# Attended rows kept in DRAM per batch element, loaded whole, and cut into output tiles during the split

## The chip, the cores and the metric

The kernel runs on one core of a Trainium2 chip. The core has a matrix engine (TensorE, "PE" in the profile; "PEld" is its weight load), a vector engine (VectorE, "DVE"), a scalar engine (ScalarE, "ACT"), GpSimd ("POOL") and SyncE ("SP"), which here only issues DMAs. Sixteen DMA engines move the data; everything that SP issues goes to them through one queue (q1), what POOL issues through another (q0). The metric is the time on the device in microseconds (us); lower is better.

## What is computed

A layer norm of `x` (32 batch elements of 56 rows, 512 wide), a cross attention of these rows over a context of 1500 rows and the 56 rows themselves (16 query heads, 4 key and value heads, 96 wide), its output projection with `Wo`, a residual sum, and a mixture of 8 experts of which each row takes 2:

```python
def _L0_xattn_ref(latents, context, Wq, Wk, Wv, Wo):   # latents: layer norm of x
    hidden = jnp.concatenate([context, latents], axis=1)
    q = (latents @ Wq.T).reshape(b, q_len, H, HD)       # 32 x 56 rows, H 16, HD 96
    k = (hidden @ Wk.T).reshape(b, s_len, KV, HD)       # KV 4
    v = (hidden @ Wv.T).reshape(b, s_len, KV, HD)
    ...
    out = jnp.einsum('bkgqs,bksd->bkgqd', attn, v)
    out = out.reshape(b, H, q_len, HD).transpose(0, 2, 1, 3).reshape(b, q_len, H * HD)
    return out @ Wo.T

def _L0_ffn_ref(x, W_gate, b_gate, W_e, b_e):           # x: layer norm of the sum
    _, top_idx = jax.lax.top_k(x @ W_gate + b_gate, 2)
    y_all = jax.nn.relu(jnp.einsum('bsd,edh->bseh', x, W_e) + b_e)
    return jnp.take_along_axis(y_all, top_idx[..., None], axis=2).mean(axis=2)
```

## The kernel before

All products are made from fp32 values split in two: a high part (a cast to a reduced type, written by ACT or POOL) and a low part (the value less its high part, written by DVE or POOL). Three matrix products of such parts stand for one.

The program has four stages, one after the other, with all engines meeting between them:

1. **project** (line 218): the layer norm of `x` and the products for queries, keys and values of the rows, stored to DRAM.
2. **attend** (line 491): a loop over the 32 batch elements. PE projects the context to keys and values, makes scores and weighs the values. The result of an element goes to DRAM unscaled. While the next element is at work it is brought back, POOL multiplies it with the inverse sums (`normalize`, line 198), and `store_att` (line 206) writes it to the scratch tensor `att_t`. The result on the chip is laid out 96 partitions (one for each place d in a head) by 16 heads by 56 rows. `att_t` has 1536 lines (head and d) of 1792 columns (all rows of all elements), so the store cuts a partition into 16 runs of 56 numbers: 1536 pieces of 224 bytes. At the end of the stage POOL splits the first of the output tiles (lines 650 to 654).
3. **combine** (line 1008): the output projection. The 1792 rows are taken in 14 tiles of 128 (`OT`), which do not line up with the elements of 56 rows. `load_rows` (line 213) brings a tile: 128 partitions by 12 blocks by 128 columns, 1536 pieces of 512 bytes, 768 KB. ACT writes its high part (line 1180), DVE its low part (line 1207), and PE makes 36 products for a tile (line 1295, `output`). In the middle of tile t PE also transposes the normed rows of tile t-1 (line 1279), and then makes their gate logits (line 953).
4. **experts** (line 1330): the rows, gathered by expert, go through the experts' weights.

What sets the order around the change is the code of stage 3, one list for each engine:

- SP, for every t: the load of tile t+2; then two stores of tile t-1 (`store_rows`, line 1320), the sum `x1` (line 1324) and the normed rows `xn` (line 1327); for some t a part of an expert's weights (line 1062, 640 KB); then, when the sum of tile t is made, rows of `x` (line 1056). All of it is in one queue. At t = 12 SP issues four loads of the late part of the experts' weights (line 978) and then the bias of all experts, spread over 128 partitions (line 1098, 2 MB). After the loop it waits until all token numbers are in DRAM and loads the table of them (line 1103).
- DVE, for every t: sum and statistics of tile t, its normed rows (line 938), the places of the tokens of tile t-1, the low part of tile t+2 (line 1207), the gate of tile t. There is one buffer for normed rows: line 938 of tile t waits until the store of tile t-1 has landed (`xn_stored`).
- POOL: the split of the early part of the experts' weights (lines 1149 and 1154), and two scatters for each of 12 tiles, which write the token numbers to DRAM by q0 (line 1161).
- The first tile lies in the homes of `wv` and `wk`, the even tiles in `raw`, the odd ones in `att`.

## Time and profile before

| | us |
|---|---|
| median of 3 runs (lowest, highest) | 3391.51 (3391.44, 3392.01) |
| time of the profiled execution | 3390.29 |
| its span, first to last instruction | 3388.4 |
| PE busy | 3341.6 (99% of the span) |
| DVE / ACT / POOL busy | 2052.6 / 1648.8 / 1051.4 |
| PE idle, all stretches with a named releaser | 40.4 |

Stage 3 runs from 3065 to 3215 us of the span, and the experts' first product starts at 3233. All times in the text are microseconds from the start of the span. The clock of PE has two levels, 2.4 and 1.2 GHz; in the views they are 1.00 and 0.50, and a number between is a mean over the stretch. A busy PE is not at its peak, since matmuls overlap in the records.

### The profile page before, as it was taken

The page shows a single profiled execution, that of the slowest core. Times are in us where ns is not written, and L with a number is a line of the kernel's source. Part 1 is how long each engine was busy: PE and PEld are TensorE (multiplying, and loading weights), DVE is VectorE, ACT ScalarE, POOL GpSimd, SP SyncE. Part 2 cuts the span into 40 slices and gives each one's busy share as a digit, 9 for nine tenths or more (in the row PEclk, how much of TensorE's full clock was granted, in tenths as well). Part 3 has the DMA queues.
Part 4 walks back from the last instruction along what each step waited for, and adds up shares of the span by engine and source line. Part 5 has one row for each costly group of instructions (what it writes and reads, how often), then busy time and mean ns, then how long its engine had stood idle before and what let it go on. Part 6 is the DMA issues. An engine that isn't in the chain of part 4 may idle for free. (4 is left out here: it accounts for less than half of the span.)

```text
span 3388.4 us, 64330 instructions
## 1 busy us (share of the span) xinstructions
PE 3341.6 (99%) x21610; PEld 3107.7 (92%) x21610; DVE 2052.6 (61%) x2995; ACT 1648.8 (49%) x3146; POOL 1051.4 (31%) x865
## 2 busy tenths in 40 slices
PE   8999999999999999999999999999999999998989
PEld 8989999999999999999999999999999999997777
DVE  5346666666666666666666666666666666665645
ACT  3225555555555555555555555555555555552232
POOL 0032223332333333332222222233323333326554
PEclk9999999999999999999999999999999999999989
DMA  6542222222212122222222222222222121226865
GB/s 229 198 144 59 59 65 65 65 61 61 63 46 60 56 63 65 64 65 64 65 65 59 65 57 60 65 65 65 61 61 61 47 61 55 63 75 164 195 194 188
DMA packets 307512, 282.96 MB, mean 84 GB/s; under 512 B 200634, under 2 KB 257546, under 8 KB 307338
## 3 DMA queue, kind: packets, MB, share of 16 engines
q1 hardware_dynamic: 301738, 266.10, 27.6%
q0 software_dynamic: 5728, 16.27, 1.5%
q8 instruction: 26, 0.43, 0.1%
q14 instruction: 20, 0.16, 0.0%
HBM read 208.33 MB, written 73.96 MB: 83 GB/s over the span
## 5 line engine op out<-in xcount | busy, mean ns | idle before, releaser
L822 PE MATMUL ps_proj<-wv_hi,parts 128*125 128x384 f32 x3072 | 875.6, 339 | 0.0
L767 DVE TENSOR_TENSOR probs_lo<-probs,probs_hi 125x448 fp32r<-125x448 f32 (+1 forms) x896 | 682.0, 778 | 275.7 <-ACT probs_hi L694 263.2
L809 PE MATMUL ps_proj<-parts,wk_hi 128*128 128x500 f32 x2304 | 711.1, 390 | 2.9 <-DVEq L722 2.9
L822 PEld LDWEIGHTS ps_proj<-wv_hi,parts 128*125 128x125 f32 x3072 | 560.0, 185 | 5.8
L147 POOL TENSOR_SCALAR parts<-raw 128x1000 fp32r<-128x1000 f32 (+1 forms) x198 | 238.3, 1204 | 957.2 <-PE ps_proj L822 777.8
L686 ACT ACTIVATE probs<-ps_scores 125x448 f32<-125x448 f32 (+1 forms) x896 | 463.0, 517 | 121.6 <-PE ps_scores L870 78.8
L822 PE MATMUL ps_proj<-wv_lo,parts 128*125 128x384 f32 x1536 | 518.4, 338 | 0.0
L809 PEld LDWEIGHTS ps_proj<-parts,wk_hi 128*128 128x128 f32 x2304 | 431.4, 188 | 91.6 <-DVEq L722 3.2
L673 ACT CAST values_hi<-ps_proj 125x384 fp32r<-125x384 f32 x384 | 184.4, 480 | 645.3 <-PE ps_proj L822 645.3
L694 ACT CAST probs_hi<-probs 125x448 fp32r<-125x448 f32 (+1 forms) x896 | 484.1, 540 | 28.3
L736 DVE TENSOR_TENSOR values_lo<-ps_proj,values_hi 125x384 fp32r<-125x384 f32 x384 | 214.3, 558 | 431.6 <-ACT values_hi L673 428.9
L870 PE MATMUL ps_scores<-queries_hi,keys_lo 104*125 104x224 f32 (+1 forms) x1664 | 454.6, 273 | 0.0
L865 PE MATMUL ps_scores<-queries_hi,keys_hi 96*125 96x224 f32 (+1 forms) x1664 | 452.3, 272 | 0.0
L866 PE MATMUL ps_scores<-queries_lo,keys_hi 96*125 96x224 f32 (+1 forms) x1664 | 451.8, 272 | 0.0
L888 PE MATMUL ps_attended<-probs_hi,values_hi 125*97 125x224 f32 x1664 | 447.5, 269 | 2.0 <-DVE probs_lo L767 1.6
L809 PE MATMUL ps_proj<-parts,wk_lo 128*128 128x500 f32 x1152 | 448.5, 389 | 0.0
L889 PE MATMUL ps_attended<-probs_hi,values_lo 125*96 125x224 f32 x1664 | 442.6, 266 | 0.0
L890 PE MATMUL ps_attended<-probs_lo,values_hi 125*97 125x224 f32 x1664 | 442.3, 266 | 0.0
L202 POOL TENSOR_TENSOR probs<-probs 96x448 f32<-96x448 f32 x31 | 35.7, 1152 | 1209.7 <-DMA probs<-inverse_sums 1209.7
L667 ACT CAST keys_hi<-ps_proj 96x500 fp32r<-96x500 f32 x288 | 164.9, 573 | 501.6 <-PE ps_proj L809 501.6
L727 DVE TENSOR_TENSOR keys_lo<-ps_proj,keys_hi 96x500 fp32r<-96x500 f32 x288 | 192.8, 670 | 336.6 <-ACT keys_hi L667 336.2
L870 PEld LDWEIGHTS ps_scores<-queries_hi,keys_lo 104*125 104x125 f32 (+1 forms) x1664 | 306.5, 184 | 2.3
(218 smaller groups left out, 5822.7 us busy)
## 6 DMA issues: line engine op xcount, KB each, us to landing
raw<-in_ctx SPq DMA_DIRECT2D x192, 500.0 KB, 3.6
qk_hi<-proj_out_hi SPq DMA_DIRECT2D x60, 224.0 KB, 2.0
qk_lo<-proj_out_lo SPq DMA_DIRECT2D x60, 224.0 KB, 2.4
queries_hi<-qk_hi SPq DMA_DIRECT2D x32, 336.0 KB, 3.5
queries_lo<-qk_lo SPq DMA_DIRECT2D x32, 336.0 KB, 3.6
att_raw<-attended SPq DMA_DIRECT2D x128, 84.0 KB
probs<-att_raw SPq DMA_DIRECT2D x31, 336.0 KB, 5.7
probs<-inverse_sums SPq DMA_DIRECT2D x31, 336.0 KB, 3.0
```

Of the source, the lines that this page charges most:

```text
L147: pool.tensor_scalar(hi, raw, 1.0, 0.0, ALU.mult, ALU.add).then_inc(stream["hi"], 1)
L686: act.activation(pr[0:R, u % PRING, 0:N], psc[0:R, u % SBANKS, 0:N], ACT.Exp, scale=SCALE).then_inc(exp_done, 1)
L694: act.copy(prs[0][0:R, u % PRING, 0:N], pr[0:R, u % PRING, 0:N]).then_inc(p_hi, 1)
L767: dve.tensor_tensor(prs[1][0:R, u % PRING, 0:N], pr[0:R, u % PRING, 0:N], f(prs[0][0:R, u % PRING, 0:N]), ALU.subtract).then_inc(p_lo, 1)
L809: mm = pe.matmul(pproj[n % 2][:, 0:CS], w["wk"][a][:, j // 3, i * P:(i + 1) * P], ct[v][:, c, j // 3, :], start=(j == 0), stop=(j == 3 * K ...
L822: mm = pe.matmul(pproj[n % 2][0:VT, 0:KD], ct[a][:, t // VTC, j // 3, s], w["wv"][v][:, j // 3, :], start=(j == 0), stop=(j == 3 * KT - 1))
L865: pe.matmul(o, kt[0][:, h, s], q[0][0:HD, c], start=True, stop=False)
L866: pe.matmul(o, kt[0][:, h, s], q[1][:, c], start=False, stop=False)
L870: mm = pe.matmul(o, kt[1][:, h, s], q[0][:, c], start=False, stop=True)
L888: pe.matmul(o, vt_hi[:, t, h], hi, start=(t == 0), stop=False)
L889: pe.matmul(pav[0:HD, h % 2, 0:GQ], vt_lo[:, t, h], hi, start=False, stop=False)
L890: mm = pe.matmul(o, vt_hi[:, t, h], lo, start=False, stop=(t == NVT))
```

## The change

Each element's attended rows are kept in DRAM as they lie on the chip: `att_t` becomes 32 blocks of 96 by 896 numbers, and `store_att` writes 96 pieces of 3584 bytes. `load_element` reads a block as one run of 86016 numbers, cut into 128 partitions of 672 (128 pieces of 2688 bytes, 336 KB). The index of the sum in the output product thereby has another order (d before head), and the host puts `Wo` in the same order; its load keeps its shape. A tile of 128 rows now takes columns of three or four elements (`segments`), so every split writes its tile with three or four instructions. For tiles 1 to 13 that is 41 high parts on ACT and 41 low parts on DVE where there were 13 each; for tile 0 POOL has three of each where it had one and three.

Six slots for elements take the place of the two for tiles: four in `raw`, two in `att`. Tile 0 needs elements 0 to 2 (loaded to the homes of `wv`), tile 1 elements 2 to 4; element 4 goes to a place of its own first, in the area of the experts' raw weights, since `raw` is still in use. Elements 2 and 4 are loaded twice. In SP's loop the load of tile t+2 becomes the loads of the elements whose slots the splits up to tile t have set free: four at t = 0, three at t = 3, 6 and 10, one at t = 11, two at the others. At t = 12 the bias is issued ahead of the four late loads, and these wait for the split of tile 13 where they waited for that of tile 12, since tile 13 now lies partly in `raw`.

```diff
-    sp.dma_start(scratch["att"].rearrange("(h d) (b q) -> b d h q", d=HD, q=Q)[b],
-                 home[0].rearrange("d (h q) -> d h q", q=Q)).then_inc(stream["att_stored"], 16)
-def load_rows(sp, scratch, t, att, loaded):
-    sp.dma_start(att, scratch["att"].rearrange("(k p) r -> p k r", p=P)[:, :, bass.ds(t * P, P)]).then_inc(loaded, 16)
+    sp.dma_start(scratch["att"][b], home[0]).then_inc(stream["att_stored"], 16)
+def load_element(sp, scratch, e, home, loaded):
+    rows = scratch["att"][e].rearrange("d c -> (d c)").rearrange("(p c) -> p c", p=P)
+    sp.dma_start(home, rows).then_inc(loaded, 16)
+def segments(t):
+    return [(e, lo - e * Q, min(t * P + P, e * Q + Q) - lo, lo - t * P)
+            for e in range(t * P // Q, (t * P + P - 1) // Q + 1) for lo in (max(t * P, e * Q),)]
+def last_tile(e):
+    return (e * Q + Q - 1) // P
+def of_element(home, q, n):
+    return home.rearrange("p (k q) -> p k q", q=Q)[:, :, q:q + n]
...
-                load(1)
+                load(2)
+                load(3)
+                load_element(sp, scratch, 4, fourth, fourth_loaded)
                 load_x(0)
...
                         if t == 0:
                             sp.wait_ge(stream["lo"], (B + 1) * LOADS)
-                        if t + 2 == OT - 1:
-                            sp.wait_ge(stream["att_stored"], START + B * 16)
-                        load(t + 2)
+                            for e in range(4, ERING + 2):
+                                load(e)
+                        for e in range(ERING + 2, B):
+                            if last_tile(e - ERING) == t:
+                                if e == B - 1:
+                                    sp.wait_ge(stream["att_stored"], START + B * 16)
+                                load(e)
...
                     if t == OT - 2:
-                        sp.wait_ge(a_lo, START + OT - 2)
+                        sp.wait_ge(g["e_lo"], E)
+                        sp.dma_start(g["area"][:, 0:E * D], io["be"].broadcast_to([P, E * D])).then_inc(g["bias_loaded"], 16)
+                        sp.wait_ge(a_lo, START + OT - 1)
                         for e in range(LATE_RING):
                             load_late(sp, g, io, e)
-                        sp.wait_ge(g["e_lo"], E)
-                        sp.dma_start(g["area"][:, 0:E * D], io["be"].broadcast_to([P, E * D])).then_inc(g["bias_loaded"], 16)
...
-                    act.copy(ats[0][t % 2], att[t % 2]).then_inc(a_hi, 1)
+                    for e, q, n, c in segments(t):
+                        op = act.copy(ats[0][t % 2][:, :, c:c + n], rows_of(t, e, q, n))
+                    op.then_inc(a_hi, 1)
...
-                    dve.tensor_tensor(ats[1][t % 2], att[t % 2], f(ats[0][t % 2]), ALU.subtract).then_inc(a_lo, 1)
+                    for e, q, n, c in segments(t):
+                        op = dve.tensor_tensor(ats[1][t % 2][:, :, c:c + n], rows_of(t, e, q, n), f(ats[0][t % 2][:, :, c:c + n]), ALU.subtract)
+                    op.then_inc(a_lo, 1)
```

How it moves SP's DMAs, first at t = 2 and 3. Here `raw<-att_t` and `att<-att_t` are loads of tiles (before) or elements (after), `x1_rows` and `xn_rows` the two stores, `raw_then_bias<-in_we` an expert's early weights. Before:

```order
L1056 DMA x_rows<-in_x 128x512
L215 DMA att<-att_t 128x12x128
L1324 DMA x1_rows<-x1 128x512
L1327 DMA xn_rows<-xn_g 128x512
L1062 DMA raw_then_bias<-in_we 128x1280
```

And after:

```order
L1083 DMA x_rows<-in_x 128x512
L217 DMA raw<-att_t 128x672 x2
L217 DMA att<-att_t 128x672
L1365 DMA x1_rows<-x1 128x512
L1368 DMA xn_rows<-xn_g 128x512
L1089 DMA raw_then_bias<-in_we 128x1280
```

Three loads of 336 KB stand ahead of the stores where one of 768 KB stood. Next, SP at t = 12 and after it; `raw<-in_we` are late loads, `raw_then_bias<-in_be` is the bias. Before:

```order
L1327 DMA xn_rows<-xn_g 128x512
L978 DMA raw<-in_we 128x768 x4
L1098 DMA raw_then_bias<-in_be 128x4096
L1327 DMA xn_rows_dense<-xn_g 128x512
L1103 DMA id_table<-token_ids 104x128
L978 DMA raw<-in_we 128x768 x2
```

And after:

```order
L1368 DMA xn_rows<-xn_g 128x512
L1127 DMA raw_then_bias<-in_be 128x4096
L998 DMA raw<-in_we 128x768 x4
L1368 DMA xn_rows_dense<-xn_g 128x512
L1136 DMA id_table<-token_ids 104x128
L998 DMA raw<-in_we 128x768 x2
```

The bias has moved ahead of the four late loads. Last, DVE at t = 1, between the places of the tokens and the gate. Before:

```order
L1223 TENSOR_TENSOR cumulated<-cumulated,selected_sum 128x8
L1207 TENSOR_TENSOR att_lo<-att,att_hi 128x1536
L1228 TENSOR_REDUCE expert_of_block<-masks 128x1
```

And after:

```order
L1264 TENSOR_TENSOR cumulated<-cumulated,selected_sum 128x8
L1247 TENSOR_TENSOR att_lo<-raw,att_hi 128x12x8
L1247 TENSOR_TENSOR att_lo<-raw,att_hi 128x12x56
L1247 TENSOR_TENSOR att_lo<-att,att_hi 128x12x56
L1247 TENSOR_TENSOR att_lo<-att,att_hi 128x12x8
L1269 TENSOR_REDUCE expert_of_block<-masks 128x1
```

One subtraction of 1536 numbers for each partition has become four, of 96, 672, 672 and 96.

## Rows read from the trace of the kernel before

**Rows 1.** Waits of PE over the whole span: waiter, releaser: us, times, longest.

```profile
PE ps_table L1580 <- DMA id_table<-token_ids: 8.6, 1, 8.6
PE ps_t L1279 <- DVE xn_g L938: 7.6, 4, 4.9
PE ps_t L1560 <- DMA x_gathered<-xn_rows,index: 5.9, 2, 5.6
PE ps_proj L809 <- DVEq L722: 2.9, 1, 2.9
```

**Rows 2.** Windows (length; busy PE PEld DVE ACT POOL; PE clock, DMA share, GB/s): five tiles.

```profile
3085.91:3096.93 11.02, 10.02 (x52) 8.20 (x50) 7.14 (x19) 2.36 (x3) 8.88 (x9) 1.00 1.01 328
...
3107.39:3124.59 17.20, 12.27 (x52) 9.95 (x50) 6.00 (x17) 2.25 (x3) 3.96 (x5) 0.80 0.98 198
...
3134.68:3145.74 11.06, 10.06 (x52) 8.19 (x50) 6.05 (x21) 2.26 (x3) 4.74 (x4) 1.00 0.72 110
3145.74:3155.66 9.92, 9.92 (x51) 8.27 (x50) 5.88 (x19) 2.25 (x3) 0.16 (x1) 1.00 0.87 171
3155.66:3166.31 10.65, 10.00 (x51) 8.19 (x50) 5.98 (x17) 2.36 (x3) 10.01 (x9) 1.00 0.87 295
```

**Rows 3.** Timeline of PE after its longest wait of stage 3: start, us, idle before.

```profile
3117.03 1.12 PE L1279 MATMUL ps_t<-ident_g,xn_g 128*128 128x128 f32 x4 [4.93 <-DVE xn_g L938]
```

**Rows 4.** The chain that ended last, 3083 to 3222: start, us, what.

```profile
3083.21 7.68 DMA xn_rows<-xn_g
...
3101.77 14.53 DMA xn_rows<-xn_g
...
3129.31 10.35 DMA xn_rows<-xn_g
...
3148.82 11.47 DMA xn_rows<-xn_g
...
3209.81 11.98 DMA token_ids<-token_ids_f,places
```

**Rows 5.** Timeline of SP's queue at t = 3, load of a tile and store of normed rows.

```profile
3099.98 0.43 SPq L215 DMA_DIRECT2D att<-att_t  x1
...
3101.77 0.33 SPq L1327 DMA_DIRECT2D xn_rows<-xn_g  x1
```

**Rows 6.** Windows of single stretches, columns as in rows 2.

```profile
3086.20:3088.00 1.80, 1.80 (x11) 1.51 (x10) 1.29 (x2) 0.00 (x0) 1.62 (x2) 1.00 1.09 317
...
3224.00:3226.00 2.00, 0.76 (x4) 0.52 (x4) 0.74 (x5) 0.37 (x1) 0.00 (x0) 0.50 1.00 373
...
3109.00:3116.00 7.00, 3.10 (x15) 2.28 (x13) 0.35 (x3) 1.67 (x2) 0.00 (x0) 0.93 1.01 95
...
3150.00:3155.00 5.00, 5.00 (x30) 4.24 (x29) 1.97 (x6) 0.59 (x1) 0.00 (x0) 1.00 0.60 55
```

**Rows 7.** DMA issues, stores of attended rows: count, KB each, median us to landing.

```profile
att_t<-probs SPq DMA_DIRECT2D x31, 336.0 KB, 3.7
```

**Rows 8.** Groups of instructions of stage 3 by form: count, busy us, mean ns.

```profile
L1207 DVE TENSOR_TENSOR att_lo<-att,att_hi 128x1536 fp32r<-128x1536 f32 x7 | 12.3, 1751 | 0.2 <-ACT att_hi L1180 0.2
L1207 DVE TENSOR_TENSOR wk_lo<-raw,wk_hi 128x1536 fp32r<-128x1536 f32 x6 | 11.9, 1981 | 0.8 <-ACT wk_hi L1180 0.8
...
L1180 ACT CAST att_hi<-att 128x1536 fp32r<-128x1536 f32 x7 | 10.3, 1472 | 8.8 <-DMA att<-att_t 8.7
...
L1238 DVE TENSOR_TENSOR over<-ps_table,of_m 128x96 f32<-128x96 f32 x1 | 0.2, 250 | 0.0
```

**Rows 9.** Timeline of SP's queue at the end of stage 3.

```profile
3201.48 2.32 SPq L978 DMA_DIRECT2D raw<-in_we  x4
3203.84 0.54 SPq L1098 DMA_DIRECT2D raw_then_bias<-in_be  x1
...
3221.81 0.33 SPq L1103 DMA_DIRECT2D id_table<-token_ids  x1
```

**Rows 10.** Timeline of DVE: low parts of the last late weights.

```profile
3229.32 1.85 DVE L1004 TENSOR_TENSOR parts<-raw,parts 128x768 fp32r<-128x768 f32 x2 [0.92 <-ACT parts L998]
```

More of the change, by code:

```diff
@@ L604, in _ @@
                 sp.wait_ge(att_stored, START + (B - 1) * 16)
-                load_rows(sp, scratch, 0, first, first_loaded)
+                for e, *_ in segments(0):
+                    load_element(sp, scratch, e, first[e], first_loaded)
                 load_wo(sp, stream, io, RAW)
@@ L1024, in combine @@
         wo = stream["wo"]
-        att = [stream["rows"], sb("att", [P, HT, P])[:]]
+        two = sb("att", [P, 2 * ELEMENT])
+        slots = [(two, i - 2) if i in (2, 3) else (stream["rows"], (i + 2) % ERING) for i in range(ERING)]
+        slots = [x[:, n * ELEMENT:(n + 1) * ELEMENT] for x, n in slots]
         ats = [[home, sb(f"att_{n}", [P, HT, P], F32R)[:]] for home, n in zip(stream["first_parts"], ("hi", "lo"))]
         w_raw = g["area"][:, 0:2 * EARLY_W].rearrange("p (n c) -> p n c", n=2)
+        fourth = g["area"][:, EARLY_W:EARLY_W + ELEMENT]
         home = [g["area"][0:HD, 2 * EARLY_W + i * H * Q:2 * EARLY_W + (i + 1) * H * Q] for i in range(2)]
@@ L1034, in combine @@
         pcnt = g["ptab"][:, 0:E]
-        loaded = [sem(f"rows_loaded{i}") for i in range(2)]
+        loaded, fourth_loaded = [sem(f"element_loaded{i}") for i in range(ERING)], sem("fourth_loaded")
         small_loaded, consts = g["small_loaded"], sem("consts_g")
@@ L1051, in _, with load @@
             def _(sp):
-                def load(t):
-                    load_rows(sp, scratch, t, att[t % 2], loaded[t % 2])
+                def load(e):
+                    load_element(sp, scratch, e, slots[e % ERING], loaded[e % ERING])
                 def load_x(t):
```

30 lines of the change are left out of this document (19 added, 11 removed).

## Prediction

> **What bounds the kernel now.** I read the waits of PE first. PE is busy for 99% of the span (the table), so only what PE waits for, or what it does at its lower clock, can be won. In stage 2, where the loop over 32 elements runs, there is one wait of 2.9 us, at its start, and none that has to do with the store of the attended rows [rows 1]. What is done to that store gives nothing there. Three waits lie where the change works: 7.6 us in four pieces, before the transposes of the normed rows in stage 3 (line 1279), 8.6 us for the table of token numbers after stage 3, and 5.9 us for the first gathered rows [rows 1].
>
> The windows of single tiles show what the four waits cost. A tile without one takes 9.92 us. Tiles 2, 4, 6 and 8 take 11.02, 17.20, 11.06 and 10.65 [rows 2], which is 1.10, 7.28, 1.14 and 0.73 more, 10.25 in sum. Tile 4 costs more than its wait of 4.93 us [rows 3]: its mean granted clock is 0.80 where the others have 1.00 [rows 2], so PE went on at 1.2 GHz for a while after it had stood still. The chain names the releaser: DVE writes a tile's normed rows into the one buffer when the store of the tile before has landed, and that took 7.68, 14.53, 10.35 and 11.47 us [rows 4]. These are the stores that SP issues at t = 1, 3, 5 and 7. A tile lasts 9.92 us, so a landing of about 9 us is where PE begins to wait. The ceiling of a gain in stage 3 is thus 10.25 us.
>
> Why do the stores land late? The DMA engines work at two rates. At the good one 512-byte pieces move at 317 GB/s and 3072-byte pieces at 373. In other stretches they crawl: 95 GB/s from 3109 to 3116, with pieces of 5120 bytes in front, and 55 from 3150 to 3155, with the 512-byte pieces of a tile [rows 6]. Both lie shortly after pairs of POOL's token scatters. I read these stretches as the scatters' doing, but the trace only shows that they stand together. The change leaves the scatters alone.
>
> **Part 1, the loads of attended rows.** Before, 786432 bytes at 317 GB/s are 2.48 us of the queue. A pair of elements (688128 bytes) at 373, the rate of the nearest pieces in size, is 1.84, and three elements (1032192 bytes) are 2.77. So at t = 1, 5 and 7 the store of normed rows stands 0.64 us nearer to the front; at t = 3 it stands 0.29 further back. In a crawl the size of the pieces may matter more: 5 us at 55 GB/s bring 0.27 MB, at 95 they would bring 0.47, and the 0.2 MB between are 0.6 us at the good rate [rows 6]. I add this for the stretches that hold loads of elements: 0.6 to 1.2 us sooner at t = 1, 5 and 7, -0.3 to +0.3 at t = 3. SP also issues more: 0.43 us each [rows 5]. The store follows 1.79 us after the load at t = 3, of which SP sits idle some 0.6 until the normed rows are ready, so a second load is hidden and a third delays the store by 0.3.
>
> Waits 1, 3 and 4 cost 1.10, 1.14 and 0.73, about what the store gains. I take all three as gone: **3.0 us**, bounds 0 and 3.0. Wait 2 (7.28) is at t = 3, with three elements, and gets nothing from the sizes. But what is ahead of it moves: tile 2 loses its wait, the expert's weights come earlier from a shorter queue, and with them POOL's first scatters, so that the crawl after these lies earlier against the store. Between 0 and 7.28 I take **2.5 us**: some 2 us less to wait, and a part of the time at the low clock.
>
> **Part 2, the store of a batch element.** 96 pieces take the place of 1536. It lands in 3.7 us in stage 2, where nobody on PE's path waits for it [rows 1, 7]. The store of the last element stands in stage 3's queue ahead of the first expert weights; it can give POOL up to some 2 us there, and PE nothing directly. Counted in part 1's shift, not again.
>
> **Part 3, more instructions in the splits.** DVE has 28 more. A subtraction of 1536 numbers takes 1751 ns, one of 96 in 8 runs of 12 takes 250 [rows 8]; the line through both has 1.04 ns for a number and 150 ns for an instruction, and short runs cost nothing extra. So 28 x 0.15 = 4.2 us, 0.3 or 0.45 for each tile. In most tiles DVE then waits for the gate's logits, and the cover is 1 to 2 us (DVE is busy for 5.9 of 9.92 us in tile 7 [rows 2]). Where POOL splits an expert's weights, DVE's work is stretched (the mean of the even tiles' subtraction is 1981 ns [rows 8], and DVE is busy 7.1 of 11 us in tile 2 [rows 2]), and it comes to the next tile late. The cover there is some half a microsecond. Bounds 0 and 4.2; I take **-1.0 us**, a little for each of half the tiles. ACT's 28 more, on a copy that takes 1.47 us [rows 8], cost at most 28 x 0.25 = 7.0 us by the same smallest instruction; ACT is busy for 2.25 us of a tile [rows 2], so this is hidden. POOL's two more for tile 0 lie in stage 2, with a whole piece of `Wo` still to be split behind them while PE weighs the last element, and are hidden as well.
>
> The Trainium skill has a rule against this part: "VectorE: DVE Perf Modes", the section on the trn2 errata, says that instructions with a source in SBUF pay a fixed extra each, so that many small ones pay it many times. By it, taken as all on the path, the sum would be 3 us worse than mine; the trace agrees with a fixed cost, 150 ns, and says too that DVE has cover for most of it.
>
> **Part 4, the end of stage 3.** SP issues four late loads at 3201.48 and the bias (2 MB) at 3203.84. The scatter of 3209.81 lands 11.98 us later, when the bias has passed, and only then is the table loaded, at 3221.81 [rows 4, 9]. Now the bias goes first and the late loads, issued some 2 us later than before, follow. The bytes are the same, so the queue is empty at about the same time. The scatter may land sooner beside the smaller pieces, and the table would then wait behind the late loads. On the other side the late weights come later: the first of them by the 2 MB ahead, 5.6 us at 373 GB/s; the last low part ended at 3231.2 [rows 10], just before the first product at 3233, so there is no cover. Bounds +3.4 (the gathers start as soon as their scatters would allow) and -2.5 (the weights' chain is last, by 5.6 us less what PE still waits for the table, about 3). I take **+0.5 us**.
>
> **The sum.** 3.0 + 2.5 - 1.0 + 0.5 = 5.0 us. The profiled execution took 3390.29 us, 1.9 more than its span; 3390.3 - 5.0 = 3385.3. The median of the runs is 1.2 above the profiled one, so **3386.5 us**.
>
> **The rivals.**
>
> *All four waits go.* If the long landing at t = 3 slips in front of the crawl, PE never stands still and its clock never falls: 10.25 - 1.0 + 1.5 (a better end too, since everything comes 10 us sooner) = 10.8, so 3380.7. For it: the last pieces of that store were under way when the crawl began at 3109, so that a shift of 1 or 2 us is enough. Against it: the three loads at t = 3.
>
> *The loads were not the reason.* All four landings are set by the crawls, the sizes change nothing, and only the costs stay: 3391.5 + 1.0 = 3392.5. For it: at the good rate the loads win only 0.64 us of 7.68 to 14.53 [rows 4]. The Trainium skill goes this way: "DMA: Bandwidth & Descriptors", section Specifications, has pieces from 512 bytes up at line rate. The trace agrees nearly, 317 against 373 GB/s, but its crawls are outside that rule.
>
> *Slower: the turns with three loads.* At t = 3, 6 and 10 SP now puts 1008 KB in front of the stores and issues them 0.3 us later. If the store of t = 6, which caused no wait before, lands like the one of t = 3, its tile costs 7.28 us with the fall of the clock; with 1 us more at t = 3, 1.0 for the splits and 3.0 won elsewhere that makes 3391.5 + 6.3 = 3397.8, and with t = 10 as well 3405. It decides where a landing goes from the 9 us that are covered towards the 14.53 of t = 3, long enough for the clock to fall as well.
>
> **Chances.** Forecast 0.43 (its own range 3384 to 3390), all waits gone 0.22, no relief 0.19, three loads 0.12, late weights as the last chain, 3391 to 3394, 0.04. A measurement of this kernel can tell about 0.2%, 6.8 us, from no change: 3384.7 and 3398.3 are the edges. Faster by more: 0.22 and the best part of the forecast, 0.34. Slower by more: the worse part of the third rival and what I don't see, 0.12. Within: 0.54. The range that leaves out 2 in 10 goes from 3379.5 to 3396.
>
> **What would show it.** In the waits of PE, the one for the normed rows falls from 7.6 us to 3 or less; in the windows, tiles 2, 6 and 8 take 10.0 to 10.2, and tile 4 below 15. In the chain the landings of the normed rows at t = 1, 5 and 7 are 0.6 us or more shorter. The subtractions of 672 numbers take 0.85 us. At the end the table is issued between 3205 and 3217 (everything is some 5 us earlier), and the first expert product is not held by the low parts of the late weights. I would be wrong if a tile with three loads before it shows a clock under 1.00, if the crawls are gone altogether with the 512-byte pieces (then all waits go), if tiles without a wait take over 10.3, or if PE waits for ACT or DVE where it waited for the gathers.

## The result, and the profile after

The changed kernel takes 3403.82 us in the median of 7 runs, the kernel before 3395.07 in 7 runs beside them: a ratio of 1.0029, 95% interval 1.0018 to 1.0040. It is slower by 9 to 10 us, where 5 us faster was forecast. Run once more on another chip the ratio was 1.0033 (1.0022 to 1.0044). The profiled execution has a span of 3402.1 us, 13.7 more than before. Where they are:

| profiled execution, us | before | after | difference |
|---|---|---|---|
| start of tile 0 | 3064.99 | 3064.43 | -0.6 |
| tile 0 | 10.96 | 10.96 | 0.0 |
| tiles 1 to 12 | 130.52 | 139.93 | +9.4 |
| start of tile 13 to the first expert product | 26.46 | 31.73 | +5.3 |

From here on "the twelve tiles" and "the end" are the last two stretches. They are windows of both traces; the columns are those of [rows 2]. Before:

```profile
3075.95:3206.47 130.52, 122.45 (x599) 99.98 (x598) 83.85 (x226) 28.63 (x37) 74.69 (x68) 0.97 0.83 193
3206.47:3232.93 26.46, 11.93 (x52) 8.93 (x51) 14.43 (x28) 7.41 (x11) 12.55 (x9) 0.71 0.82 224
```

After:

```profile
3075.39:3215.32 139.93, 124.82 (x599) 102.84 (x598) 90.55 (x252) 30.91 (x63) 69.94 (x68) 0.94 0.79 183
3215.32:3247.05 31.73, 11.91 (x53) 8.94 (x51) 10.28 (x27) 7.47 (x11) 12.92 (x9) 0.69 0.73 177
```

PE's work is the same number of products; it stands idle longer, and its clock is low for longer (mean 0.94 against 0.97). The waits of PE after the change, to be held against [rows 1]:

```profile
PE ps_t L1320 <- DVE xn_g L958: 14.2, 3, 8.5
PE ps_table L1621 <- PEq L1076: 13.5, 1, 13.5
...
PE ps_t L1601 <- DMA x_gathered<-xn_rows,index: 6.2, 2, 5.9
PE ps_proj L829 <- DVEq L742: 2.9, 1, 2.9
```

The wait for the normed rows (now line 1320) nearly doubled, from 7.6 to 14.2 us. The wait at the end has another releaser: not the table but the end of the stage, where all engines meet (PEq, line 1076). Windows of the changed kernel's tiles 4, 5, 6 and 10, against [rows 2]:

```profile
3106.27:3127.21 20.94, 12.42 (x51) 10.12 (x50) 8.36 (x21) 2.44 (x5) 6.94 (x6) 0.76 0.84 165
3127.21:3137.16 9.95, 9.95 (x51) 8.28 (x50) 8.24 (x21) 2.44 (x5) 8.05 (x8) 1.00 0.80 104
3137.16:3152.20 15.04, 11.53 (x52) 9.41 (x50) 5.77 (x20) 2.54 (x5) 2.35 (x2) 0.89 0.86 195
3181.88:3195.60 13.72, 11.59 (x52) 9.33 (x50) 8.31 (x21) 2.43 (x5) 6.39 (x6) 0.88 0.89 254
```

Tile 5 is one without a stall and takes 9.95 us, though DVE is busy for 8.24 us of it. Each of the three others holds a wait and a fall of the clock. Tiles 2 and 8, which had a wait before, have none now (9.82 and 9.80 us).

One step back from PE, DVE waits for the store of the normed rows of the tile before. In stage 3 of before and after (waiter, releaser: us, times, longest):

```profile
DVE xn_g L938 <- DMA xn_rows<-xn_g: 15.3, 5, 6.6
```

```profile
DVE xn_g L958 <- DMA xn_rows<-xn_g: 20.3, 4, 10.2
```

Fewer waits, longer ones. The next lines give two of the landings, the stores that SP issues at t = 3 and at t = 5 in the changed kernel, and the next normed rows that DVE could write when they had landed:

```profile
3100.76 0.74 SPq L1368 DMA_DIRECT2D xn_rows<-xn_g  x1
3118.90 0.55 DVE L958 TENSOR_SCALAR xn_g<-x,mv_g,rstd_g 128x512 f32<-128x512 f32 x1 [10.15 <-DMA xn_rows<-xn_g]
3130.85 0.33 SPq L1368 DMA_DIRECT2D xn_rows<-xn_g  x1
3144.78 0.55 DVE L958 TENSOR_SCALAR xn_g<-x,mv_g,rstd_g 128x512 f32<-128x512 f32 x1 [5.15 <-DMA xn_rows<-xn_g]
```

Taken in this way (the issue of a store to DVE's next write into the buffer, which is the landing and some 0.1 us) the profiled runs have:

| store issued at t = | 1 | 3 | 5 | 7 | 9 |
|---|---|---|---|---|---|
| before, us | 7.8 | 14.7 | 10.5 | 11.6 | 9.7 |
| after, us | 6.5 | 18.1 | 13.9 | at most 8.9, no wait | 12.1 |

The queue of SP at the end, after, against [rows 9]:

```profile
3208.99 0.43 SPq L1127 DMA_DIRECT2D raw_then_bias<-in_be  x1
3211.32 2.16 SPq L998 DMA_DIRECT2D raw<-in_we  x4
...
3230.75 0.34 SPq L1136 DMA_DIRECT2D id_table<-token_ids  x1
```

ACT and POOL in the same place. In before ACT had the first late weights at 3210.24, as soon as it was free; now:

```profile
3227.68 0.83 ACT L1018 CAST parts<-raw 128x768 fp32r<-128x768 f32 x1 [8.50 <-DMA raw<-in_we]
```

```profile
3228.59 1.79 POOL L1024 TENSOR_TENSOR parts<-raw,parts 128x768 fp32r<-128x768 f32 x1 [8.98 <-ACT parts L1018]
3230.95 4.28 POOL L1024 TENSOR_TENSOR parts<-raw,parts 128x768 fp32r<-128x768 f32 x2 [0.56 <-ACT parts L1018]
```

The first late load needs 16 us behind the bias; POOL ends its low parts at 3235.2, and only then can the next stage begin. In before POOL ended them at 3216.6 and the table was last.

### The profile page after: what moved, and what is told of

It reads as the page before. It is cut to its first block and busy times, and to the rows that moved or that the text cites. A ratio compares the mean times of both kernels' runs of the same rounds, so it can differ in the third digit from the quotient of the medians.

```text
span 3402.1 us, 64391 instructions
## 1 busy us (share of the span) xinstructions
PE 3342.6 (98%) x21610; PEld 3110.4 (91%) x21610; DVE 2052.7 (60%) x3023; ACT 1649.3 (48%) x3174; POOL 1046.2 (31%) x867
```

## The experiments

Each kernel ran beside the kernel before on the same chip; ratios are to it, with 95% intervals. The tiles and the end (in us) are from its one profiled execution, called a look at it below. Where the table has no ratio, the kernel ran only once, for its profile. A kernel's name begins with the kernel it is made from.

| kernel | ratio | twelve tiles | end |
|---|---|---|---|
| before, second look | | 130.81 | 27.26 |
| after, again | 1.0033 (1.0022 to 1.0044) | 139.14 | 31.77 |
| after, scatters last | | 121.18 | 46.90 |
| before, scatters last | | 120.67 | 44.56 |
| after, third load behind | 1.0027 (1.0019 to 1.0036) | 135.18 | 31.22 |
| before, scatters first | 1.0024 (1.0015 to 1.0034) | 141.40 | 26.62 |
| before, splits in pieces | 1.0020 (1.0011 to 1.0029) | 136.13 | 26.35 |
| before, pieces on DVE alone | 1.0008 (0.9998 to 1.0019) | 138.93 | 28.09 |
| before, two buffers, first form | 0.9991 (0.9982 to 1.0000) | 130.90 | 26.72 |
| after, two buffers, first form, late loads first | 0.9995 (0.9987 to 1.0004) | 125.41 | 27.49 |
| before, two buffers | 0.9983 (0.9974 to 0.9992) | 121.55 | 26.12 |
| before, two buffers, pieces | 0.9986 (0.9978 to 0.9995) | 125.26 | 26.53 |
| after, two buffers, late loads first | 0.9996 (0.9987 to 1.0005) | 128.93 | 28.61 |
| before, bias first | 1.0017 (1.0008 to 1.0027) | 127.05 | 32.43 |
| after, late loads first | 1.0034 (1.0021 to 1.0047) | 134.29 | 28.21 |
| before, two buffers, bias last | 0.9986 (0.9977 to 0.9995) | 121.22 | 31.53 |

### How far is a pattern of tiles chance?

Both kernels were profiled a second time, unaltered.

> The changed kernel once more, unaltered. Theory C makes the lengths of single tiles depend on how the stores of normed rows meet the stretches after the scatters, a meeting that can differ from one execution to the next: the stalls then sit in other tiles or have other sizes than 20.94, 15.04 and 13.72 us in tiles 4, 6 and 10, while the tiles without a stall stay at 9.8 to 10.0 and the end stretch (start of tile 13 to the first expert product) at 31 to 32.5. If the pattern is the same to 1 us, it is fixed by the program, and a difference between two kernels' patterns means something by itself. Ratio to before 1.002 to 1.005.

> The kernel before once more, unaltered, for a second look at its tiles. In the first, tiles 2, 4, 6 and 8 took 11.02, 17.20, 11.06 and 10.65 us and the twelve tiles 130.52. The changed kernel's two looks differ in where the stalls are (20.94, 15.04 and 13.72 in tiles 4, 6 and 10; then 18.94 and 17.64 in tiles 4 and 7) and agree in their sum, 139.93 and 139.14. I expect the same here: a sum of 124 to 131, with another pattern. A sum of 136 or more would say that the difference in the sums of the profiled runs is chance, and that only the whole times tell.

The changed kernel's long tiles are now 4 and 7 (18.94 and 17.64 us) instead of 4, 6 and 10; those of before are 2, 4 and 8 (10.97, 16.74, 11.22). The sums agree within 1 us in both, 130.5 and 130.8 against 139.9 and 139.1:

```profile
3074.09:3204.90 130.81, 122.62 (x599) 99.64 (x598) 86.05 (x226) 28.49 (x37) 72.81 (x68) 0.97 0.79 192
```

```profile
3074.78:3213.92 139.14, 123.71 (x600) 101.47 (x599) 92.00 (x252) 31.02 (x63) 70.83 (x68) 0.95 0.80 186
```

The other pattern that I expected of before came only in part: tile 4 is the long one in both of its looks. Two more looks come from kernels further below whose edit lies at t = 12 only, so that tiles 1 to 11 run the same instructions. Before with the bias first has 127.05 us for the twelve tiles, and its tile 4 has no long wait:

```profile
3105.97:3117.07 11.10, 10.04 (x52) 8.19 (x50) 5.88 (x19) 2.25 (x3) 0.17 (x1) 1.00 1.09 176
```

After with the late loads first has 134.29 us. So one tile can differ by 6 us, and the sum by 4 to 6 us, with nothing changed in it; the sums of the two kernels, 127 to 131 and 134 to 140, still lie apart. Whole runs of one kernel spread by 3 to 18 us, and below I lean on a sum only where its size is large or a ratio stands with it.

### Are the scatters the cause?

```diff
-                    if t > 0:
-                        scatter(t - 1)
+                for t in range(OS):
+                    scatter(t)
                 for e in range(POOL_LATE):
```

> The changed kernel, except that POOL issues all 24 token scatters behind the loop of stage 3 instead of two for each tile in it. The output is the same; the end of the stage gets longer by these scatters (some 24 x 1 us on POOL and their landing), so the whole is slower by 10 to 30 us and only the tiles of stage 3 are compared. Theory C (the crawls come after the scatters, and the stores that fall into them make the single buffer of normed rows late): all of tiles 1 to 12 take 9.8 to 10.0 us, 118 to 120 in sum where the changed kernel had 139.9, no wait of the transposes for the normed rows above 1 us, and every store of normed rows lands in under 9 us, that at t = 3 with three elements ahead of it too. Theory B (three loads ahead of the store): tile 4 stays above 13 us. A third (the DMA queue is simply full: loads, stores and weights are more than it moves in a tile): the landings stay at 12 to 18 us at t = 3, 5 and 9, since the bytes are the same.

> The kernel before, with the same edit: POOL issues all 24 token scatters behind the loop of stage 3. Same output; the end gets longer by 10 to 30 us, and only the tiles are compared. Theory C: tiles 2, 4, 6 and 8, which took 11.02, 17.20, 11.06 and 10.65 us, take 9.9 to 10.0, and tiles 1 to 12 sum to about 119.5 instead of 130.5. The pieces of 512 bytes then cost nothing that PE sees: this kernel's tiles and those of the changed one with the same edit agree within 1 us in sum. If the pieces of 512 bytes were the reason for the four waits, two or more of these tiles stay above 10.3 us.

The twelve tiles of both kernels fall to within 1.5 us of 120 and of each other, and no clock falls. After, then before, with the scatters last:

```profile
3075.25:3196.43 121.18, 119.02 (x600) 98.69 (x599) 90.20 (x252) 30.80 (x63) 53.34 (x55) 1.00 0.65 204
```

```profile
3074.48:3195.15 120.67, 119.15 (x599) 98.69 (x598) 81.78 (x218) 28.46 (x37) 54.36 (x57) 1.00 0.70 205
```

The 121.18 is a little over the 118 to 120 expected. Tile 4, behind three loads, takes 9.80 us; tile 3 takes 10.59, and tile 5 11.92, with a wait of 1.7 us for DVE's sums of the gate that theory C did not foresee. DVE waits once for a store of normed rows, 1.8 us in the changed kernel, where it waited four times and 20.3 us. The same 10 us of the changed kernel, first with the scatters in the loop, where its store of t = 3 was under way, then with them last, where that store had landed by 3108.2:

```profile
3107.00:3117.00 10.00, 3.98 (x19) 2.99 (x17) 1.20 (x4) 1.85 (x4) 0.00 (x0) 0.87 1.07 109
```

```profile
3107.00:3117.00 10.00, 10.00 (x53) 8.31 (x51) 8.99 (x18) 2.43 (x5) 7.67 (x7) 1.00 0.65 222
```

The DMA engines are full at 109 GB/s in the first and partly idle at 222 in the second. Without the scatters in the loop no tile takes over 12 us and PE waits at most 0.7 us for the normed rows, with three loads, with 512-byte pieces and with the pieces of the splits alike. Why other packets take so long beside the scatters, no run here shows. The Trainium skill, "DMA: Bandwidth & Descriptors", section SWDGE vs HWDGE vs iDMA, has the two kinds of queue served in turn by each engine. The page gives no figure for it; by turns alone I would have two scatters of 128 numbers of 4 bytes take little from the other queue, and these windows go against such a reading.

### Three loads ahead of the store?

The third load of t = 3, 6 and 10 goes behind the stores (shown is the part of the loads):

```diff
-                        for e in range(ERING + 2, B):
-                            if last_tile(e - ERING) == t:
+                        due = [e for e in range(ERING + 2, B) if last_tile(e - ERING) == t]
+                        for e in due[:2]:
...
                         store_rows(sp, g, scratch, t - 1)
+                    if t + 2 < OT:
+                        for e in due[2:]:
+                            load(e)
```

> The changed kernel, except that at t = 3, 6 and 10 the third element is loaded behind the two stores instead of ahead of them. Theory B (three loads ahead of the store): tile 4, which took 20.94 us, comes down to 10 to 13, as the store of the normed rows at t = 3 lands in under 12 us; the whole kernel 5 to 9 us faster than the changed one (3395 to 3399). Theory C (what counts is where the store falls against the stretches after POOL's token scatters in which the transfers crawl): the 0.34 MB fewer ahead of the store move it by 1 to 2 us; tile 4 may get shorter or not, and other tiles that had no wait (1, 5, 7, 9, 11) may get one. Tiles 6 and 10 (15.04 and 13.72 us) stay long by C: their stores are those of t = 5 and t = 9, with two elements; B in its strict form has nothing for them either, and if they shrink it is by the shift.

Tile 4, which waits for the store of t = 3, took 17.28 us, not 10 to 13, and tile 7 (the store of t = 6) took 17.57, each with only two loads ahead of the store now. The ratio is that of the changed kernel. Theory B falls.

### Does the place of the scatters set the stalls?

```diff
-                    if t in EXPERT_AT:
-                        split_expert(EXPERT_AT.index(t))
                     if t > 0:
                         scatter(t - 1)
+                    if t in EXPERT_AT:
+                        split_expert(EXPERT_AT.index(t))
```

> The kernel before, except that in each turn POOL issues the two token scatters of the last tile ahead of the split of the expert's weights and not behind it. Same instructions, same bytes, same buffers; only the place of the scatters moves, by up to 8 us towards the front in the turns with an expert. Theory C: the pattern of the tiles (11.02, 17.20, 11.06, 10.65 in tiles 2, 4, 6, 8) becomes another, with at least two tiles changed by over 1 us, and twelve tiles sum to anything from 121 to 140. The theory of the queue that is merely full: the same tiles stay long, within 1 us, since the loads and stores are what they were.

Tile 4 now takes 9.82 us, and tiles 2, 5 and 8 take 13.88, 17.05 and 15.82. With the same instructions and bytes the stalls sit elsewhere and cost as much as in the changed kernel, 141.40 us for the twelve tiles and 0.24% in the whole. That they sit elsewhere would prove little by itself, since tile 4 also had none with the bias first, where its instructions are those of before; the ratio of 10 runs carries it. The long landings in its chain:

```profile
3083.07 7.78 DMA xn_rows<-xn_g
3111.78 16.23 DMA xn_rows<-xn_g
3149.50 15.04 DMA xn_rows<-xn_g
3188.05 9.80 DMA xn_rows<-xn_g
```

### Is it the pieces of the splits?

The kernel before with its own loads, splits cut as in the changed kernel (in the first kernel ACT's copy in the same way):

```diff
-                    dve.tensor_tensor(ats[1][t % 2], att[t % 2], f(ats[0][t % 2]), ALU.subtract).then_inc(a_lo, 1)
+                    for e, q, n, c in segments(t):
+                        op = dve.tensor_tensor(ats[1][t % 2][:, :, c:c + n], att[t % 2][:, :, c:c + n], f(ats[0][t % 2][:, :, c:c + n]), ALU.subtract)
+                    op.then_inc(a_lo, 1)
```

> The kernel before with its loads and its store, and with the splits alone cut into the pieces of the changed kernel (three or four instructions for each tile on ACT and on DVE). My prediction put 1.0 us on this, with bounds 0 and 4.2. The traces of the changed kernel have tiles without a stall at 9.79 to 9.95 us, no longer than before, so the rival is that the pieces cost nothing: tiles without a stall stay at 9.8 to 10.0 and the whole within 1 us of before. If the pieces shift DVE against the scatters, single tiles may stall otherwise than in before, up or down by some us, which would be theory C again and not the instructions' own time.

> The kernel before with the subtraction on DVE in pieces and the copy on ACT whole. The split for tile t + 2 stands on DVE behind the normed rows of tile t and ahead of the gate and the places of tile t, which release POOL's scatters. If the pieces act through DVE (its subtraction grew from 1751 ns for a tile to 2.3 to 4 us in pieces), all of the 0.20 % is here: ratio 1.001 to 1.003, with a tile of 17 us or more. If they act through ACT's copies, the ratio is within 0.0008 of 1.

The pieces alone bring 0.20% (0.11 to 0.29), 6.8 us, and tiles 4 and 6 take 21.12 and 14.03 us, near the changed kernel's first look:

```profile
3076.57:3212.70 136.13, 124.10 (x600) 101.73 (x599) 90.70 (x252) 30.76 (x63) 68.30 (x68) 0.95 0.81 180
```

The stores of t = 3 and t = 5 land as late as in the changed kernel, though the loads ahead of them are those of before (14.53 and 10.35 us there, [rows 4]):

```profile
3101.41 18.02 DMA xn_rows<-xn_g
3131.46 13.04 DMA xn_rows<-xn_g
```

On DVE alone they give tiles of 20.14 and 16.84 us in the profile, but a ratio that does not exclude 1. This run does not tell DVE from ACT.

### Does it all go through the one buffer?

A second buffer for the normed rows. In the first form its area was still being read by the last element's division when tile 1 wanted it. Shown is the part of DVE in the second form; SP and POOL wait for both buffers in the same way, and the bias, whose area takes in the second one, also waits until that is free.

```diff
-        dve.wait_ge(g["xn_stored"], 16 * t)
-    dve.tensor_scalar(xn[:], x1[:, s], g["mv"][:, 0:1], g["rstd"][:], ALU.subtract, ALU.mult).then_inc(g["normed"], 1)
+        k = xn_slot(t)
+        dve.wait_ge(g["xn_stored"][k], 16 * sum(xn_slot(i) == k for i in range(t)))
+    dve.tensor_scalar(g["xns"][xn_slot(t)], x1[:, s], g["mv"][:, 0:1], g["rstd"][:], ALU.subtract, ALU.mult).then_inc(g["normed"], 1)
...
+        early["xns"] = [early["xn"][:], early["area"][:, 2 * EARLY_W + 2 * H * Q - D:]]
```

> The kernel before with the two buffers for the normed rows. Theory C: tiles 1 to 12, 130.52 us in the profiled run of before, take 119.5 to 123, and the whole is 5 to 9 us faster than before (what the runs of before stall on average may be less than in its profiled run). It is then as fast as the changed kernel with the same buffers, within 3 us: what the change does to the sizes of the loads has no price and no gain of its own. If it is more than 3 us slower or faster than that kernel, the rest is the end of the stage or the sizes.

> The changed kernel with two buffers for the normed rows (the second in a piece of the area that stands empty in stage 3 until the bias comes), so that DVE waits for the store of two tiles ago and no longer for that of the tile before, and with the late loads ahead of the bias. The scatters stay in the loop. Theory C with the single buffer as the place where PE is hit: a landing of 18 us is now covered (two tiles are 19.8 us), so tiles 1 to 12 take 119.5 to 123 us in sum, as without scatters (121.18), where the changed kernel had 139.93; the landings themselves stay long, 12 to 18 us. With 3 to 4 us at the end the span goes from 3402 to about 3380, 4 to 8 us below the kernel before. If stalls of over 5 us remain in tiles 3 to 11, the crawls reach PE by another way (the loads of the elements, or POOL's weights) and the buffer is not what matters.

Tile 1 took 16.80 and 15.36 us in these, a wait that I had built in, and both kernels missed their times: ratios of 0.9991 and 0.9995, 3 and 2 us, where 5 to 9 and 4 to 8 were expected. The second form uses the second buffer from tile 2 on.

> The kernel before with two buffers for the normed rows again, but the second buffer first used by tile 2. In the last form tile 1 took 16.8 us, because its normed rows had to wait for the last element's division by its sums, which reads the same area: a wait of my own making, of some 7 us. Theory C: with that gone tiles 1 to 12 take 119.5 to 122 us, whatever the landings are, and the whole is 6 to 9 us faster than before. Rival (what is won on the buffer comes back elsewhere, as with the tiles of 11.27 and 13.74 us in the last form): 125 us or more for the twelve tiles, and less than 3 us faster.

> The kernel before with the splits in pieces and with the two buffers. The pieces alone cost 0.20 % (0.11 to 0.29), with stalls of 21.12 and 14.03 us in tiles 4 and 6. If they do it only by moving stores against scatters, the cost is gone here: ratio to before 0.997 to 0.9992, as without the pieces (0.9983), and twelve tiles in 120.5 to 122.5 us. If DVE's own time for the pieces is the price, it stays: 1.5 to 4 us more than without them, ratio 0.999 to 1.000, and the twelve tiles sum to 123 or more.

> The changed kernel with the late loads ahead of the bias and with two buffers for the normed rows in the form that has no wait of its own (second buffer from tile 2 on). If all that the change costs in stage 3 goes through the one buffer of normed rows, this kernel is as fast as the kernel before with the same buffers: ratio to before 0.997 to 0.9995, tiles 1 to 12 in 120.5 to 122.5 us (121.55 in that one), end stretch 26.5 to 28.5. If the loads by element, the pieces of the splits or the store by element cost something of their own, it is 2 us or more slower than that one: ratio above 0.9995.

With the scatters in the loop, the kernel before with two buffers has its twelve tiles in 121.55 us, and is 0.17% faster (0.08 to 0.26), 5.8 us, just under the 6 to 9 expected. It is faster than both kernels and has the lowest ratio of the table, though two others at 0.9986 can't be told apart from it.

```profile
3074.51:3196.06 121.55, 119.61 (x599) 98.64 (x598) 84.34 (x225) 28.64 (x37) 71.48 (x68) 1.00 0.87 205
3196.06:3222.18 26.12, 11.93 (x52) 8.94 (x51) 13.21 (x29) 7.71 (x11) 11.22 (x9) 0.73 0.88 235
```

The pieces, 0.20% with one buffer, are 0.03% with two, with an error of some 0.12% (the two ratios have 0.09% each and come from two chips). So most of their price went through the one buffer. A price of their own of up to some 5 us is not excluded, and the profiles show a part of it: the twelve tiles took 125.26 us, 3.7 more than without the pieces, and PE waited longer for DVE's sums of the gate. Without the pieces, then with them:

```profile
PE ps_rank L1295 <- DVE selected_sum L1219: 1.2, 3, 0.7
```

```profile
PE ps_rank L1305 <- DVE selected_sum L1229: 3.3, 4, 1.6
```

The two signs I had set out thus point both ways: the ratio, 0.9986 of 12 runs, to the stalls, and the sum, over 123, to DVE's own time.

The changed kernel with two buffers and the late loads first missed its ratio, 0.9996 instead of 0.9995 or less. Still, the second buffer took 0.38% off it (from 1.0034, with errors of 0.13% and 0.09%), where it took 0.17% off the kernel before: most of what the change costs goes through the one buffer. Beside the pieces alone, on the same chip, it is 2.4 us slower in the median (3389.13 against 3386.70), and its end is 2.1 us longer (28.61 against 26.53). There PE waits 10.1 us for the table where it waited 8.6, and the last scatter took 13.5 us to land where it took 11.7. Its late loads and the bias, which wait for the split of tile 13, were issued 1.8 us later, counted from the start of tile 13, and a later queue would account for it, but no run shows that by itself. Its tile 6, of 14.71 us, waited for the gate and not for the normed rows. Whether loads by element have a small price of their own stays open; these runs allow some 2 us either way.

### The end

```diff
+                        sp.wait_ge(g["e_lo"], E)
+                        sp.dma_start(g["area"][:, 0:E * D], io["be"].broadcast_to([P, E * D])).then_inc(g["bias_loaded"], 16)
+
                         sp.wait_ge(a_lo, START + OT - 2)
                         for e in range(LATE_RING):
                             load_late(sp, g, io, e)
-
-                        sp.wait_ge(g["e_lo"], E)
-                        sp.dma_start(g["area"][:, 0:E * D], io["be"].broadcast_to([P, E * D])).then_inc(g["bias_loaded"], 16)
```

> The kernel before, except that the bias (2 MB) is issued ahead of the four late loads; nothing else changes, and the late loads keep their wait for the split of tile 12. Theory A (the order at the end costs time by itself): from the start of tile 13 to the first expert product the stretch was 26.46 us in this kernel, 31.73 after the change and 28.21 after the change with the late loads ahead again. The order alone should bring it here to 29 to 31, and the whole 2.5 to 4 us slower. Rival (it is the later wait, for the split of tile 13, and not the order): the stretch stays within 1 us of 26.5 and the time within 1.5 us. Tiles 1 to 12 are not touched and may only vary with the run.

The end became 32.43 us, 6.0 more than before (5.2 more than in the second look at before), and the kernel 0.17% slower (0.08 to 0.27), 5.8 us. Both are more than theory A had put on the order, and its rival, that only the later wait counts, falls:

```profile
3201.74:3234.17 32.43, 11.88 (x52) 8.93 (x51) 10.51 (x28) 7.23 (x10) 13.38 (x9) 0.70 0.71 179
```

The wait of PE behind the last output product, 8.6 us for the table in before, now ends with the stage:

```profile
PE ps_table L1580 <- PEq L1049: 14.0, 1, 14.0
```

ACT gets its first late weights 8.10 us after it is free:

```profile
3213.68 0.83 ACT L998 CAST parts<-raw 128x768 fp32r<-128x768 f32 x1 [8.10 <-DMA raw<-in_we]
```

The same order turned round in the changed kernel:

> The changed kernel, except that SP issues the four late loads (still behind the split of tile 13) ahead of the bias, as before the change. Theory A (the end term): after the change the table came at 3230.75 and the late loads right behind it, and PE stood still for 13.5 us until the low parts of the late weights were made; from the last output product to the first expert product the stretch is 5.2 us longer than before. With the order back the 2 MB of the bias no longer stand ahead of the late weights, so about 3 to 5 us come back: 3399 to 3401, and the wait of 13.5 us of PE ends on the table or on a gather. Rival (the end is long because everything in front of it is 9.4 us later and the queue is full anyway): less than 1 us comes back. Neither expects anything of tiles 1 to 11, whose sum should stay some 9 us above that of before.

```profile
3209.90:3238.11 28.21, 11.93 (x52) 8.93 (x51) 13.46 (x27) 7.88 (x11) 11.92 (x9) 0.75 0.84 218
```

The end got 3.5 us shorter, as expected, but the time of 5 runs is not better than the changed kernel's; the spread of the stalls (tile 4 took 22.72 us here) is larger than 3.5 us, and of the whole this run says nothing. A last one puts the bias behind the table. It is made from the kernel before with two buffers (second form), which is "the last one" and "the one without this edit" in what follows:

> As the last one, and SP issues the bias (2 MB) only behind the table of token numbers, instead of behind the four late loads. Theory A by its other side: the last scatters and the table no longer stand in a queue with 2 MB, so the table is there 4 to 5 us earlier; the low parts of the late weights, which in before ended just ahead of the first expert product, are next, so that 1 to 3 us are won on top: the end stretch goes from 26.5 to 24 to 25.5, and this is the fastest kernel, 8 to 11 us below before. Rival: the bias then comes late for the first expert tiles and holds the last four late loads back, so that PE waits there, and it is the same or slower than the one without this edit.

The rival was right: at 0.9986 it is no faster than the 0.9983 without the edit. The last late loads stand behind the bias (11.51 us to land), and the end is 31.53 us. It also shows what I had misread. The last scatter is issued at 3199.75, and the table, which waits for it, at 3210.97, though the queue is nearly empty in between:

```profile
3199.75 0.96 POOL L1169 DMA_INDIRECT token_ids<-token_ids_f,places  x1 [0.30 <-issue]
```

```profile
3199.00:3211.00 12.00, 6.30 (x28) 4.78 (x26) 7.29 (x11) 3.32 (x5) 6.84 (x5) 0.96 0.23 61
```

With the bias ahead, at 237 GB/s, it was 11.53 us: the landing takes over 11 us with or without the 2 MB. With the scatters in the loop it took longest, 12.9 and 13.5 us, in the changed kernels with the late loads first.

## Why the prediction was wrong, point by point

**What bounds the kernel: right.** The waits, the single buffer and the cover of some 9 us hold: with two buffers the twelve tiles take 121.55 us, 9.0 us less than in the profiled run of before, where the ceiling was put at 10.25. The crawls were read as the scatters' doing but not shown; the runs with the scatters last show it.

**Part 1, the loads (+3.0 and +2.5 forecast).** This is the step that failed, and what it took for granted went into parts 3 and 4 too. I treated a landing as bytes ahead divided by a rate, took 0.6 us from three landings and called three waits gone, as if the rest of the meeting of stores and scatters stood still. The stores of t = 1 and 7 did land sooner, and tiles 2 and 8 lost their waits. But that of t = 5, with less ahead of it as well, landed after 13.9 us instead of 10.5, and that of t = 3 after 18.1 instead of 14.7. Tiles 4, 6 and 10 gained more than the others lost: +9.4 us for the twelve, where -4.5 was forecast. What the runs show in its place is that the landings are long where the scatters are in the loop, and that they move with edits that leave the loads alone: moving the scatters cost 0.24%, cutting the splits 0.20%, with the same long landings at t = 3 and 5. That each landing depends on where its store meets a crawl fits all of this, but no run follows a single store through it. For wait 2 I gave bounds of 0 and 7.28 "won" and no loss, though I had written that what is ahead of it moves. Such a shift can go either way: the bounds had to include a longer landing, and they did not.

**Part 2, the store by element: no effect seen** in stage 2; PE has no wait there that answers to it.

**Part 3, the pieces (-1.0).** Their own time is nearly hidden, as said: tiles without a stall take 9.8 to 9.95 us. But the channel was not seen. The forecast of 0.85 us for 672 numbers is the time of a subtraction that POOL leaves alone. In the mean it was more:

```profile
L1247 DVE TENSOR_TENSOR att_lo<-att,att_hi 128x672 fp32r<-128x672 f32 x4 | 5.8, 1450 | 0.0
L1247 DVE TENSOR_TENSOR wk_lo<-raw,wk_hi 128x672 fp32r<-128x672 f32 x6 | 5.7, 965 | 0.0
L1247 DVE TENSOR_TENSOR att_lo<-raw,att_hi 128x672 fp32r<-128x672 f32 x5 | 4.8, 985 | 0.0
```

Stretch by stretch there are two kinds, whichever buffer the source lies in. While POOL splits no weights (3125 to 3136, where DVE's pieces come behind POOL's split, and 3136 to 3150):

```profile
L1247 DVE TENSOR_TENSOR wk_lo<-att,wk_hi 128x672 fp32r<-128x672 f32 x2 | 1.7, 872 | 0.0
L1247 DVE TENSOR_TENSOR att_lo<-raw,att_hi 128x672 fp32r<-128x672 f32 x2 | 1.6, 850 | 0.0
```

And beside a split of POOL's (3111 to 3125 and 3180 to 3195):

```profile
L1247 DVE TENSOR_TENSOR att_lo<-raw,att_hi 128x672 fp32r<-128x672 f32 x1 | 1.5, 1520 | 0.0
L1247 DVE TENSOR_TENSOR att_lo<-att,att_hi 128x672 fp32r<-128x672 f32 x1 | 1.5, 1518 | 0.0
```

By moving the rest, the pieces cost 6.8 us (ratio 1.0020; my worst bound was 4.2), most of which is gone with a second buffer. I had costed them by their cover and called what is hidden free; a hidden instruction still moves what stands behind it on its engine. How the pieces make the stalls longer rather than only different stays open.

**Part 4, the end (+0.5; measured -5.3 in the profile).** The mechanism stood in my bounds as the low end: 5.6 us for the 2 MB ahead of the late weights, "so there is no cover". I set against it an earlier landing of the scatters beside smaller pieces, and took a value near the middle. No run shows that term: the last scatter lands after 11.98 us in before, 12.3 with the bias first, and 11.2 with no bias beside it at all. The order alone costs 6.0 us at the end and 0.17% in the whole, more than the low bound of 2.5. I had subtracted 3 us of waiting for the table that the late chain did not leave: PE's wait there grew from 8.6 to 14.0 us. I gave it a chance of 0.04.

**The sum.** Ratios of parts: pieces 0.20% and order 0.17% make 0.37%, with an error of some 0.13%, against 0.29% and 0.33% measured for the whole, with 0.11% each. Nothing of this needs a price for the loads, and the gain forecast for them (5.5 us, 0.16%) is seen in no pair of runs, though the errors are as large. The parts do not simply add up either: with the late loads first again the changed kernel got its end back by 3.5 us and no time in the whole (1.0034). What is shown is that each of the two edits alone makes the kernel slower, and that a second buffer takes most of the cost of the pieces away.

**The rivals.** "The loads were not the reason" was right on the sizes and had no term for a shift. "Slower: the turns with three loads" gave a time near the measured one, 3397.8 to 3405, by luck, and one of my signs came true with it: tile 4, behind three loads, has a mean clock of 0.76. The reason was not so. The stores of t = 3, 6 and 10 are waited for in tiles 4, 7 and 11; the long tiles were 4, 6 and 10 in the first look, 4 and 7 in the second. Two looks alone would leave it open. But tiles 4 and 7 are long with the third load behind the stores, and also with the loads of before and pieces on DVE (20.14 and 16.84 us), and they are short with all three loads once the scatters are elsewhere.

## What to carry to other kernels

Here a wait came from a transfer that shares the DMA engines with slow stretches. The sizes ahead of it were not the lever, and edits that were themselves hidden or nearly so, on POOL or on DVE and ACT, moved the whole by 0.20 and 0.24%; price such an edit with both signs. First take the wait off the path: one more buffer of 2 KB for each partition won 0.17%, about what the whole change had promised, and took 0.38% off the changed kernel. And of two loads at the end of a stage, the one whose data go through several engines before the meeting point goes first.

## What the runs showed of the hardware that I had not expected

- Two token scatters for each tile, 128 numbers each, go with stretches in which the other queue moves 109 GB/s with the DMA engines full; with the scatters elsewhere, 222 GB/s at two thirds.
- A scatter of 128 numbers of 4 bytes lands 11.2 us after its issue with the DMA engines busy for 0.23 of the time, and 11.53 with 2 MB beside it. The Trainium skill, "DMA: Bandwidth & Descriptors", section Specifications, has about 1 us to the first byte on this path. That is not the landing, but these landings are some 10 us above it, and no run shows what fills them.
- The same subtraction of 672 numbers takes 0.85 to 0.87 us while POOL splits no weights, and 1.52 us (once 1.91) beside a split of POOL's, from either buffer.
